# Position rows of 2,112 columns built in halves of 64 rows, with padded operand rows and a regrouped TensorE step

## The reference

```python
q = heads(x @ Wq + bq); k = heads(x @ Wk + bk); val = heads(x @ Wv + bv)
pos = (_sinusoid_pos_emb(S, D) @ Wp + bp).reshape(S, H, P).transpose(1, 0, 2)
content_score = jnp.einsum('bhsp,bhtp->bhst', q + u, k)
pos_score = jnp.einsum('bhsp,htp->bhst', q + v, pos)
pos_score = _relative_shift(pos_score)     # pad one column on the left, reshape to (s + 1, s), drop the first row
score = (content_score + pos_score) / jnp.sqrt(jnp.float32(P))
weights = jax.nn.softmax(score, axis=-1)
out = jnp.einsum('bhst,bhtp->bhsp', weights, val)
```

## Time and profile before

| | us |
|---|---|
| median of 3 runs | 10139.81 |
| lowest and highest run | 10116.28, 10143.54 |
| the profiled execution's own time | 10126.49 |
| its span, first to last instruction | 10124.7 |

### The profile page before, as it was taken

How to read it: one execution, slowest core, us unless ns; L and a number is a source line. 1 busy time by engine, 2 the same in 40 slices (tenths; PEclk the granted TensorE clock), 3 DMA queues, 4 the chain that set the end, 5 groups by cost and what they waited for, 6 DMA issues and landing times. The chain is left out here.

```text
span 10124.7 us, 255387 instructions
## 1 busy us (share of the span) xinstructions
PE 8878.6 (88%) x91488; PEld 5861.3 (58%) x91488; DVE 5925.2 (59%) x12530; ACT 5848.2 (58%) x10811; POOL 2788.2 (28%) x2894
## 2 busy tenths in 40 slices
PE   5888889799788888989978888898997888889899
PEld 3666666445466666644546666664554666666345
DVE  4666664564466666457446666645745666663673
ACT  4766774454476676445447666644545666763454
POOL 2333332100233333210033333321003333332101
PEclk8999999899899999989989999998998999999899
DMA  7999993210699999321079999922107999992210
GB/s 271 404 393 392 406 407 154 67 35 25 259 403 389 388 404 398 142 68 35 24 280 405 394 394 401 395 114 71 32 25 307 402 388 392 406 398 93 66 36 23
DMA packets 439117, 2552.01 MB, mean 252 GB/s; under 512 B 59008, under 2 KB 89216, under 8 KB 175360
## 3 DMA queue, kind: packets, MB, share of 16 engines
q1 hardware_dynamic: 437760, 2534.40, 63.9%
HBM read 1284.53 MB, written 1248.85 MB: 250 GB/s over the span
## 5 line engine op out<-in xcount | busy, mean ns | idle before, releaser
L815 POOL TENSOR_SCALAR z<-z,nmax 128x1024 f32<-128x1024 f32 x2048 | 2277.9, 1123 | 3718.2 <-DVE nmax L764 3718.2
L754 DVE CUSTOM_DVE_ANT_0 z<-sc,z 128x1024 f32<-128x1024 f32 x2048 | 2497.4, 1220 | 1370.1 <-DMA z<-rel_rows 1038.5
L727 ACT ACTIVATE pT<-rg 128x512 f32<-128x512 f32 x4096 | 2449.0, 598 | 715.7 <-PE rg L635 656.1
L635 PE MATMUL rg<-ident,z 128*128 128x128 f32 x16384 | 2523.4, 277 | 58.6 <-issue 51.5
L635 PEld LDWEIGHTS rg<-ident,z 128*128 128x128 f32 x16384 | 1976.5, 142 | 742.3 <-ACT rel L735 296.6
L735 ACT ACTIVATE rel<-rg 128x512 f32<-128x512 f32 x3072 | 1721.9, 596 | 1157.5 <-PE rg L602 638.7
L1065 ACT ACTIVATE pT<-rg 128x512 f32<-128x512 f32 (+3 forms) x2560 | 1226.2, 530 | 830.2 <-PE rg L997 499.9
L602 PE MATMUL rg<-pos_s,qv_s 96*128 96x512 bf16 (+3 forms) x2560 | 908.1, 361 | 614.5 <-DVE rel L789 610.7
L1081 DVE TENSOR_REDUCE mx_b<-sc 128x1 f32<-128x1024 f32 (+7 forms) x1024 | 1004.2, 991 | 527.0 <-PE sc L979 290.0
L656 PE MATMUL op<-pT,xnT 128*32 128x128 f32 x32768 | 1130.2, 279 | 0.0
L656 PEld LDWEIGHTS op<-pT,xnT 128*32 128x32 f32 x32768 | 847.7, 111 | 247.5 <-issue 154.5
(11 more groups left out here) (115 smaller groups left out, 9099.0 us busy)
## 6 DMA issues: line engine op xcount, KB each, us to landing
rel_rows<-rel SPq DMA_DIRECT2D x1024, 1088.0 KB, 8.7
z<-rel_rows SPq DMA_DIRECT2D x1024, 1024.0 KB, 9.2
v_heads<-rel SPq DMA_DIRECT2D x8, 4096.0 KB, 12.6
xnT<-v_heads SPq DMA_DIRECT2D x128, 256.0 KB, 4.4
qu_parts<-z SPq DMA_DIRECT2D x36, 512.0 KB
pos_s<-pos_parts SPq DMA_DIRECT2D x64, 192.0 KB, 9.1
qv_parts<-z SPq DMA_DIRECT2D x24, 512.0 KB
k_parts<-z SPq DMA_DIRECT2D x24, 512.0 KB
```

The costliest lines, as they stand in the source:

```text
L635: mm = e.transpose(rg[:, T_BANK[q], (j - 4 * q) * P:(j - 4 * q + 1) * P], z[:, n % RING, j * P:(j + 1) * P], ident[:, :])
L727: e.activation(pT[:, t % 2, q * CH:(q + 1) * CH], rg[:, T_BANK[q], :], ACT.Exp, scale=SCALE).then_inc(p_ready[q], 1)
L754: e.tensor_tensor_reduce(out=zs, in0=scf[:, 2 * half * CH:2 * (half + 1) * CH], in1=zs, scale=1.0, scalar=-3.0e38, op0=ALU.add, op1=ALU.ma ...
L815: e.tensor_scalar(zs, zs, 1.0, nmax[:, n % 2:n % 2 + 1], ALU.mult, ALU.add).then_inc(AA[done], 1)
```

## The change

1. A row of `rel` and of `rel_rows` has 2112 columns in place of 2176: the skew is made for blocks of 64 queries, so the tail has 64 columns. Each piece of the position rows is now made by two matmuls of 64 stationary columns that write PSUM partitions 0 to 63 and 64 to 127; where a piece holds the edge between row i and row i + 1, by four.
2. The skewed read of a tile is two transfers of 64 rows x 2048 in place of one of 128 x 2048, and the wait for it counts both.
3. The operand tensors in DRAM are laid out as (part, head, feature, line) with lines of 2176 bf16, of which 2048 are used. The store of a part is now one view of 128 rows x 2048.
4. PE's step is put in another order, so that work with 64 stationary columns stands in two places: pieces 1, 2 and the next step's 3 together, and piece 0 with the tail. ACT and DVE follow: ACT copies piece 0 between the exponentials, DVE copies piece 3 ahead of the first half of the scores and the tail ahead of the second.

```diff
+LINE = S + 128
 SLOTS = 6
 KROWS = SLOTS * HD
-W = S + P
+SH = P // 2
+W = S + SH
...
-        qu_d = nc.dram_tensor("qu_parts", (H, PARTS * HD, S), BF16).ap()
-        qv_d = nc.dram_tensor("qv_parts", (H, PARTS * HD, S), BF16).ap()
-        k_d = nc.dram_tensor("k_parts", (H, PARTS * HD, S), BF16).ap()
-        pos_d = nc.dram_tensor("pos_parts", (H, PARTS * HD, S), BF16).ap()
+        qu_d = nc.dram_tensor("qu_parts", (PARTS, H, HD, LINE), BF16).ap()
+        qv_d = nc.dram_tensor("qv_parts", (PARTS, H, HD, LINE), BF16).ap()
+        k_d = nc.dram_tensor("k_parts", (PARTS, H, HD, LINE), BF16).ap()
+        pos_d = nc.dram_tensor("pos_parts", (PARTS, H, HD, LINE), BF16).ap()
...
-                hs = dst[m * (H // KT):(m + 1) * (H // KT), :, :].rearrange("h (a d) s -> a h d s", a=PARTS)
+                hs = dst[:, m * (H // KT):(m + 1) * (H // KT), :, :].rearrange("a h d s -> a (h d) s")
                 for i in range(PARTS):
-                    e.dma_start(hs[i], parts[j % SETS][i]).then_inc(pj_stored[j % SETS], 16)
+                    e.dma_start(hs[i, :, 0:S], parts[j % SETS][i]).then_inc(pj_stored[j % SETS], 16)
...
-                hd, i0 = n // NT % NB, n % NT * P
-                edge = min(max(i0 + P - c * CH, 0), CH)
-                if edge > 0:
-                    j0 = PAD + S - P - i0 + c * CH
-                    mm = e.matmul(rg[:, R_BANK[c], 0:edge], qv_s[hd][:, i0:i0 + P], pos_b[hd][:, j0:j0 + edge],
-                                  start=True, stop=True)
-                if edge < CH:
-                    j0 = PAD + c * CH + edge - i0 - P - 1
-                    mm = e.matmul(rg[:, R_BANK[c], edge:CH], qv_s[hd][:, i0 + 1:i0 + P + 1],
-                                  pos_b[hd][:, j0:j0 + CH - edge], start=True, stop=True)
+                hd = n // NT % NB
+                blocks = [(g, n % NT * P + g * SH) for g in range(P // SH)]
+                edges = [min(max(i0 + SH - c * CH, 0), CH) for _, i0 in blocks]
+                for (g, i0), edge in zip(blocks, edges):
+                    if edge > 0:
+                        j0 = PAD + S - SH - i0 + c * CH
+                        mm = e.matmul(rg[g * SH:(g + 1) * SH, R_BANK[c], 0:edge], qv_s[hd][:, i0:i0 + SH],
+                                      pos_b[hd][:, j0:j0 + edge], start=True, stop=True)
+                for (g, i0), edge in zip(blocks, edges):
+                    if edge < CH:
+                        j0 = PAD + c * CH + edge - i0 - SH - 1
+                        mm = e.matmul(rg[g * SH:(g + 1) * SH, R_BANK[c], edge:CH], qv_s[hd][:, i0 + 1:i0 + SH + 1],
+                                      pos_b[hd][:, j0:j0 + CH - edge], start=True, stop=True)
                 mm.then_inc(r_full[c], 1)
...
-                j0, m = PAD + S - i0 - P - 1, min(P, S - i0 - 1)
-                e.matmul(tail[0:m, :], qv_s[hd][:, i0 + 1:i0 + 1 + m], pos_b[hd][:, j0:j0 + P],
-                         start=True, stop=True).then_inc(tail_full, 1)
+                for g in range(P // SH):
+                    i0 = n % NT * P + g * SH
+                    j0, m = PAD + S - i0 - SH - 1, min(SH, S - i0 - 1)
+                    mm = e.matmul(tail[g * SH:g * SH + m, :], qv_s[hd][:, i0 + 1:i0 + 1 + m],
+                                  pos_b[hd][:, j0:j0 + SH], start=True, stop=True)
+                mm.then_inc(tail_full, 1)
...
-            e.dma_start(k[first:last:2, :], k_src[bass.ds(h, 1), i * HD:(i + 1) * HD, :]
-                        .rearrange("a (r d) s -> (a d) r s", d=HD).to_broadcast([HD, reps, S])).then_inc(done, 16)
+            e.dma_start(k[first:last:2, :], k_src[i:i + 1, bass.ds(h, 1), :, 0:S]
+                        .rearrange("r a d s -> (a d) r s").to_broadcast([HD, reps, S])).then_inc(done, 16)
...
-                shifted = bass.AP(tensor=rel_d.tensor, offset=hd * FLAT + i0 * W + P - 1, ap=[[W - 1, P], [1, S]])
-                e.dma_start(z[:, k, :], shifted).then_inc(rel_in[k], 16)
+                for g in range(P // SH):
+                    shifted = bass.AP(tensor=rel_d.tensor, offset=hd * FLAT + (i0 + g * SH) * W + SH - 1,
+                                      ap=[[W - 1, SH], [1, S]])
+                    e.dma_start(z[g * SH:(g + 1) * SH, k, :], shifted).then_inc(rel_in[k], 16)
```

More of the change, by code:

```diff
@@ L91 @@
 ROWS = dict(bv=0, bo=1, Bbv=2, Bbo=3, b2=4)
-Counts = namedtuple("Counts", "tiles fours moves pairs values")
+Counts = namedtuple("Counts", "tiles fours moves pairs values reads")
 Marks = namedtuple("Marks", "heads blocks pieces groups pairs values rows steps")
@@ L190, in program @@
         po = op[:, 0:P]
-        tail = op[:, 2 * P:3 * P]
+        tail = op[:, 2 * P:2 * P + SH]
         on = op[:, P:P + OB * VW].rearrange("p (o w) -> p o w", o=OB)
@@ L663, in step @@
                 began = s >= 0
+                if here(r):
+                    if began or r >= 1:
+                        e.wait_ge(r_copied[0], base.tiles + r)
+                    rows_of(p, base, r, 3)
+                if here(c):
+                    content(p, base, c, 0, not began and c == 0)
                 if here(t):
@@ L670, in step @@
                     turn(t, 0)
-                if here(c):
-                    content(p, base, c, 0, not began and c == 0)
-                if here(t):
                     if here(r - 1):
@@ L678, in step @@
                     turn(t, 1)
+                if here(c):
+                    content(p, base, c, 1, not began and c == 0)
                 if here(r):
-                    if began or r >= 1:
-                        e.wait_ge(r_copied[0], base.tiles + r)
-                    rows_of(p, base, r, 3)
+                    e.wait_ge(r_copied[3], base.tiles + (r + 1))
+                    rows_of(p, base, r, 0)
+                    if here(v - 1):
+                        e.wait_ge(AA["po_copied"], base.tiles + v)
+                    row_tail(base, r, not began and r == 0)
                 if here(t):
@@ L686, in step @@
                     turn(t, 2)
-                if here(c):
-                    content(p, base, c, 1, not began and c == 0)
-                if here(t):
                     e.wait_ge(p_ready[1], base.tiles + (t + 1))
                     turn(t, 3)
-                if here(r):
-                    e.wait_ge(r_copied[3], base.tiles + (r + 1))
-                    rows_of(p, base, r, 0)
                 if here(s):
-                    e.wait_ge(tail_copied, base.tiles + (r if here(r - 1) else G))
+                    e.wait_ge(tail_copied, base.tiles + (r + 1 if here(r) else G))
                     combine(p, base, s)
+                if here(v):
+                    if not here(s):
+                        e.wait_ge(tail_copied, base.tiles + (r + 1))
+                    values(p, base, v)
                 if here(r):
@@ L703, in step @@
                     rows_of(p, base, r, 1)
-                    row_tail(base, r, not began and r == 0)
-                if here(v):
-                    values(p, base, v)
-                if here(r):
                     if here(t):
@@ L724, in step @@
                         e.wait_ge(AA["pv_done"], base.tiles + (t - 1))
-                    for q in range(4):
-                        e.wait_ge(t_full[q], base.tiles + (t + 1))
-                        e.activation(pT[:, t % 2, q * CH:(q + 1) * CH], rg[:, T_BANK[q], :], ACT.Exp,
-                                     scale=SCALE).then_inc(p_ready[q], 1)
+                    probabilities(0)
+                    probabilities(1)
                 if here(r):
@@ L732, in step @@
                         e.wait_ge(rel_out[r % RING], moved(base, r - RING))
+                    rows_out(R_MID)
+                if here(t):
+                    probabilities(2)
+                    probabilities(3)
+                if here(r):
                     for c in R_ACT:
[L734 to L736 removed]
+                        if c != R_MID:
+                            rows_out(c)
             in_order(e, b, step)
@@ L781, in step @@
                 first = s < 0 and c < 2
-                if here(c):
-                    score(p, base, c, 0, first)
                 if here(r):
@@ L791, in step @@
                 if here(c):
+                    score(p, base, c, 0, first)
+                if here(r):
+                    e.wait_ge(tail_full, base.tiles + (r + 1))
+                    e.tensor_copy(rel[:, r % RING, S:W], tail).then_inc(tail_copied, 1)
+                if here(c):
                     score(p, base, c, 1, first)
@@ L796, in step @@
                     e.tensor_copy(po_sb[:, v % OB, :], po).then_inc(AA["po_copied"], 1)
-                if here(r):
-                    e.wait_ge(tail_full, base.tiles + (r + 1))
-                    e.tensor_copy(rel[:, r % RING, S:W], tail).then_inc(tail_copied, 1)
                 if here(s) and s % OB == OB - 1:
```

24 lines of the change are left out of this document (16 added, 8 removed).

## The result

| | before | changed |
|---|---|---|
| median of 4 runs each, us | 10138.53 (10116.28 to 10143.54) | 10952.86 (10911.72 to 10974.69) |
| ratio, 95% interval | | 1.080 (1.077 to 1.084) |
| profiled execution: own time, span, us | 10126.5, 10124.7 | 10974.69, 10972.9 |
| granted clock of TensorE, mean of the span | 0.954 | 0.931 |
| steady tile of attention A, us (below) | 5.70 | 6.64 |

The changed kernel is 8.0% slower; the forecast of 9950 us is off by 1000 us, and the time lies where the prediction put the rival "the halves collide", between its +0.6 us a tile and the end of the range.

A forecast was written before the change was run, and what follows sets the result against it. Attention A was taken as bound by the DMA engines at 5.67 us a tile. 10126.5 - 83 (bytes) - 101 (stores) = 9942 us, given as 9950 us; forecast's own range 9715 to 10070, range given up to 11200 us.

The forecast's parts named there:

- the halves collide: Rival, attention A's read: halves into 64 partitions get half the rate, +2.5 us a tile, 12500 us in all; chance 0.27.
- Bytes of the position rows: Attention A: write falls from 1088 to 1056 KB a tile, -83 us; read stays 1024 KB, its second transfer costs nothing.
- operand stores: Projections: stores go from half to all DMA engines, -101 us in all, bounds 0 and -138 us.
- padded lines: Operands in DRAM: rows of 4352 instead of 4096 bytes; nothing taken beyond the bytes, -312 us with them as low end.
- PE's order: PE's step in attention A: three changes take it from 5.21 to 5.3 us, under the DMAs' 5.59, nothing on the path.
- (a): PE's step: piece 3 is copied ahead of the scores, so 0.36 us of waiting before piece 0 goes.
- (b): PE's step: narrow work changes width five times instead of two, +0.45 us, bounds 0 to +0.6.
- (c): PE's position products: two matmuls on two halves of the columns, side by side, cost as one.
- The page's line of slices: Whole run: about 24 of 40 slices have a DMA share of 9 tenths, four blocks of six, read as attention A.
- PE becomes the bound: Rival, attention A: a piece's halves run one after the other, 6.2 us a tile, 10570 us with the stores; chance 0.10.
- the stores stay slow: Rival, projections: only the bytes count, 10045 us; one end of the forecast, inside its chance of 0.60.
- the floor: Rival: padding gives all of its bound and PE stays at 5.3 us, 9713 us; an end of the forecast's 0.60.

The follow-up runs named there:

- e2: Kernel before, with the position rows read in two transfers by halves of columns, both covering all 128 partitions: 10167.6 us, ratio 1.004.
- e1: Kernel before, with the position rows read in two transfers of 64 rows, into partitions 0 to 63 and 64 to 127: 11176.5 us, ratio 1.103.
- e3: Changed kernel with one plain read of 128 rows, the second half's own offset left out (output wrong): 9915.8 us, ratio 0.980 to the kernel before.
- e11: Changed kernel with the write of the position rows queued between the two half reads: 11901.6 us, ratio 1.175 to the kernel before.
- e6: Kernel before with the new padded operand layout and the new order of PE, ACT and DVE, one read of 128 rows: 9968.9 us, ratio 0.984.
- e8: Changed kernel with half reads on even and odd partitions and the rest put in that order, nothing left out: 9900.5 us, 0.977 of the kernel before.
- e10: e6 with each position product made as two of 64 columns: 9988.4 us, ratio 0.987 to the kernel before.
- e5: Kernel before with only the change's operand layout, part first with padded rows, its stores and loads: 9983.6 us, ratio 0.986.
- e9: e5 without the padding, rows of 2048 columns in place of 2176: 9985.0 us, ratio 0.987 to the kernel before.
- e7: Kernel before with only the new order of PE's, ACT's and DVE's step, operands laid out as before: 10116.0 us, ratio 0.999.
- e12: Changed kernel with its two reads made as one transfer whose source has two levels of rows: 27417.2 us, ratio 2.708 to the kernel before.
- e4: Changed kernel with its half reads landing on even and odd partitions, row order not restored (output wrong): 9906.2 us, 0.979 of the kernel before.

## Why the prediction was wrong

**The step that failed** is in "Bytes of the position rows": the read "stays at 1024 KB. It becomes two transfers", priced at an issue and 16 completion packets, "I take nothing for these." Issue and packets are indeed worth little (e2: +0.04 us a tile). But the read was taken to keep its rate, and it doesn't: each transfer into 64 neighbouring partitions runs slower. The split alone costs +1050 us in e1, +1.03 us a tile, and without it the changed kernel falls by 1037 us (e3). The prediction had the mechanism, as a rival at 0.27, with 2.5 us a tile as its whole price, and held three things against it. That the load with 16 partitions was quick and that the halves follow at once told nothing of engines that work on the same half at the same time. (Nor was there much in the row held for it, 3.1 us for 128 KB against 2.8 for 192 KB: the `z<-k_parts` loads of the same sizes land in 2.8 and 3.1 us, the other way about.) That writes lie between two reads, so that engines out of step don't meet, isn't borne out: e11 has a write on either side of each half, and pays more. And though the prediction allowed anything between none and the whole price, it counted mostly on a collision that is there in full or not at all, while by its own figure any price over 0.18 us a tile was enough to turn the sign.

The other steps, by run:

| step | forecast | measured | by |
|---|---|---|---|
| bytes of the write | -83 us | -68, -88 | e6 to e8, e10 to e8 |
| operand stores | -101 us | -147 us | e5 |
| padded lines | 0 | 0 | e5 against e9 |
| PE's order, (a) | 0 on the path | -14 us | e7 |
| PE's halves and widths, (b) and (c) | 0 on the path | +20 us, at the edge of the noise | e10 against e6 |
| the read in halves | 0 | +1050, +1037 us | e1, e3 |

The terms add up: 10130 - 147 (e5) - 15 (e6) + 20 (e10) - 88 (e8) = 9900, which is e8. So far they are differences from one run to the next and must close; the test is that e1's 1050 us, measured in the kernel before, lead from there to 10950, and the changed kernel takes 10953.

- **Operand stores**: right mechanism, size too small by 46 us. An A pass gained 16 us and a B pass 15 where 12 and 11.5 were forecast. That is about what the last operand wait lost: in each of the two stages it fell to 17 us a pass, from 35 and 33, where 20 were forecast. Stores within the projections land earlier too: ACT's wait for one fell from 58.9 to 33.2 us in 4, 6.4 us each where 3.9 were taken. The start before the first write gained 23.7 us, where 7 for the position operands and 12 were forecast. The bound of -138 us was wrong: "all of the waits' 34 us" in one stage is 277.7 / 2 = 139, but the wait stands in two stages a pass.
- **PE's order**: PE's own step is 5.28 us in e8 and 5.3 was forecast, but by luck. 5.21 - 0.36 = 4.85 us was taken for the new order and 0.45 us for the widths; measured are 5.10 us (e6) and 0.10 us more with the halves (e10), and the weave gives most of the rest in e8. Both terms were too large, and cancelled. Two halves side by side cost 0.41 against 0.39 us, as (c) says. The late read moved from piece 0 to `combine`, behind the tail's copy, as the prediction said. It also said that PE feels only what is late by more than about 1 us: over 120 tiles the scores waited 230.9 us and PE 107.7, so 1.0 us a tile was not felt.
- **The page's line of slices**: "about 24" slices at 9 tenths are 20; the first of each block of six is at 6 or 7. Nothing hangs on it.
- **PE becomes the bound** fell by e10, **the stores stay slow** by e5, and **the floor** by e9.
- **What would show it wrong** was "a DMA share near 1.0 with a rate well below 400 GB/s in attention A": 1.00 at 337.

## What to carry to other kernels

When a transfer to all 128 partitions is cut, look at which partitions each piece reaches, not only at its bytes and its number: pieces by columns (395 against 402 GB/s) or on alternate partitions (397) keep the rate or nearly, pieces of 64 neighbouring partitions (337) lose it. A DMA share of 1.0 is no sign that the rate is whole; read the GB/s beside it. If a layout forces halves by rows, weave them over the partitions and undo the weave where a transpose reads an identity anyway, which here cost 4 to 6 ns a transpose and some split operations in the projection, and won 1050 us.

## What the runs showed of the hardware that was not expected

- The price of two half reads depends on what stands between them: +1.03 us a tile with the halves back to back, +1.94 us with a write of 1056 KB between them (full price 2.50).
- One transfer whose source has two levels of rows, 2 x 64, runs at 99 GB/s in all, as if two engines carried the read; the same 128 rows with one step run at the rate of 396 GB/s.
- With the transfers slower TensorE's granted clock is lower: 0.99 in e8's steady stretch, 0.94 in the changed kernel, 0.90 in e11 and 0.65 in e12, each a mean over times at its two levels, 1.2 and 2.4 GHz. PE waited more in each, and its busy time for the same work rose from 9127 us (e4) to 9520 us (changed) and 11553 us (e12). I don't take it for a cause here: in the changed kernel and in e11 the DMA share is 1.00, and the packets of the read are longer themselves.
